# Graph attention stack on one core: layer 1's transposed input in another PSUM bank, and the context of layers 4 and 5 as three products of high and low halves

## What is computed

```
scores = where(adj == 0, -inf, q @ k.T * scale)
attn   = softmax(scores)
x      = layer_norm(x + (attn @ v) @ w + b) * gamma + beta
```

## Time and profile before

| | |
|---|---|
| median of 3 runs | 2370.72 us (2369.71 to 2372.63) |
| profiled execution, its own time | 2373.87 us |
| its span, first to last instruction | 2372.1 us |
| PE busy | 2259.9 us, 95% of the span |
| PE weight loads busy | 2136.2 us, 90% |
| DVE busy | 1783.3 us, 75% |
| POOL busy | 1794.9 us, 76% |
| ACT busy | 1620.0 us, 68% |
| mean granted TensorE clock | 0.990 of full speed |
| DMA | 68.78 MB, mean 29 GB/s |

### The profile page before, as it was taken

The page is one execution under the profiler, slowest core; times in us unless marked ns, Lnnn a source line. Parts: engine busy times, 40 slices in busy tenths (PEclk is TensorE's granted clock), DMA queues, the critical chain, the costliest instruction groups (busy, mean ns, idle before and its releaser), DMA issues.

```text
span 2372.1 us, 59576 instructions
## 1 busy us (share of the span) xinstructions
PE 2259.9 (95%) x20624; PEld 2136.2 (90%) x20624; DVE 1783.3 (75%) x7734; ACT 1620.0 (68%) x5515; POOL 1794.9 (76%) x2399
## 2 busy tenths in 40 slices
PE   6899999999999999999999999999999999999985
PEld 5799999999999999999999999999999999999974
DVE  4777777777877877877877877877777777777864
ACT  5667767767767767767767767766766766767742
POOL 3368878878878878878878878878878878878751
PEclk9999999999999999999999999999999999999998
DMA  4000000100110000010010000000010010000000
GB/s 154 20 23 24 30 28 24 30 28 25 29 28 25 29 28 26 28 28 26 28 28 27 27 28 28 26 28 28 26 28 28 26 28 28 26 29 17 15 10 14
DMA packets 38747, 68.78 MB, mean 29 GB/s; under 512 B 4400, under 2 KB 12848, under 8 KB 37936
## 3 DMA queue, kind: packets, MB, share of 16 engines
q1 hardware_dynamic: 38448, 64.97, 9.0%
HBM read 48.18 MB, written 16.78 MB: 27 GB/s over the span
## 4 chain that ended last, share of the span: by engine, by line
PE 80%; DVE 9%; ACT 7%; issue 2%; POOL 1%; DMA 0%; POOLq 0%; SPq 0%; DVEq 0%
PE value_bank L450 17%; PE qk_bank L442 16%; PE context_bank L595 9%; PE unit_bank L450 7%; PE unit_bank L442 7%; PE qk_bank L549 7%; PE score_bank L579 5%; ACT probs L676 5%; PE unit_bank L506 4%; PE unit_bank L518 3%; DVE scores L820 2%; PE score_bank L576 2%; PE score_bank L586 2%; DVE xT_lo L854 2%; DVE scores L860 1%
## 5 line engine op out<-in xcount | busy, mean ns | idle before, releaser
L1046 POOL TENSOR_TENSOR x<-y,rows 128x512 f32<-128x512 f32 x305 | 392.0, 1285 | 188.9 <-DVE y L913 188.9
L698 ACT CAST xT_hi<-qk_bank 128x512 fp32r<-128x512 f32 x320 | 187.7, 587 | 399.8 <-PE qk_bank L549 399.6
L676 ACT ACTIVATE probs<-scores,negmax 128x128 f32<-128x128 f32 x1024 | 399.1, 393 | 88.6 <-DVE negmax L820 88.6
L913 DVE TENSOR_SCALAR y<-y,mv,rstd 128x256 f32<-128x256 f32 x730 | 304.2, 459 | 191.6 <-POOL rstd L1030 191.3
L442 PE MATMUL qk_bank<-xT_hi,w_lo 128*128 128x256 f32 x1280 | 411.5, 321 | 21.6 <-DVE xT_lo L854 21.3
L1054 POOL TENSOR_TENSOR x<-x,rows 128x512 f32<-128x512 f32 x305 | 393.8, 1291 | 19.2
L450 PE MATMUL value_bank<-w_lo,xT_hi 128*128 128x256 f32 x1280 | 394.4, 308 | 0.0
L442 PE MATMUL qk_bank<-xT_lo,w_hi 128*128 128x256 f32 x1280 | 363.5, 284 | 0.0
L442 PE MATMUL qk_bank<-xT_hi,w_hi 128*128 128x256 f32 x1280 | 362.1, 283 | 0.0
L450 PE MATMUL value_bank<-w_hi,xT_lo 128*128 128x256 f32 x1280 | 361.8, 283 | 0.0
L450 PE MATMUL value_bank<-w_hi,xT_hi 128*128 128x256 f32 x1280 | 361.0, 282 | 0.0
(11 more groups left out here) (93 smaller groups left out, 6503.3 us busy)
## 6 DMA issues: line engine op xcount, KB each, us to landing
x0T<-xT_in SPq DMA_DIRECT2D x64, 256.0 KB, 3.0
x<-x_in SPq DMA_DIRECT2D x64, 256.0 KB, 3.0
out<-x_out SPq DMA_DIRECT2D x64, 256.0 KB, 2.3
adj<-adj_in SPq DMA_DIRECT2D x64, 128.0 KB, 2.2
late_weights<-w_in SPq DMA_DIRECT2D x2, 1024.0 KB, 7.1
rows<-rows_in SPq DMA_DIRECT2D x1, 1792.0 KB, 11.7
probs0T<-w_in SPq DMA_DIRECT2D x4, 256.0 KB, 4.2
x<-w_in SPq DMA_DIRECT2D x1, 1024.0 KB, 13.2
```

The lines of the kernel that those rows point to most:

```text
L676: e = act.activation(probs0[:, j, g, quad], scores0[:, j, g, quad], ACT.Exp, scale=-1.0, bias=negmax0[:, j, g, quad:quad + 1], accum_out=t ...
L913: m = dve.tensor_scalar(y[:, r, g], y[:, r, g], mv[:, r, g, 0:1], rstd[:, r, g:g + 1], ALU.subtract, ALU.mult)
L1046: pool.tensor_tensor(result(norm), y[:, NORM_AT[norm] % YS], row_of_each(f"gamma{layer}"), ALU.mult).then_inc(zg_ready, 1)
```

## The change

Two parts. First, layer 1's input is transposed into `unit_bank[0]` instead of `qk_bank`, so `transpose_x` for layer 1 no longer waits for `qk_ready`; it waits for DVE's first `row_max0` of the next group, which reads that bank. ACT's copy to `xT` becomes a step of its own, `move_xT`, behind `softmax`, and DVE's `split_lo` no longer waits for it. Second, the context of layers 4 and 5 is made of three fp32r products per graph. For this ACT's two copies, of v and of probsT, write the high halves, and DVE gets two new subtractions per item for the low halves: `split_v` (128x512) and `split_probsT` (128x256). PE's waits for v and probsT become waits for the low halves.

The core of the diff:

```diff
+def in_halves(i):
+    return item(i)[0] >= LAYERS - 2
...
+        def xT_bank(i):
+            return unit_bank[0] if item(i)[0] == 1 and NTH[i] > 0 else qk_bank
...
             def transpose_x(i):
                 layer, group = item(i)
                 wait_result(pe, source_of(i))
-                if NTH[i] > 0:
+                psum = xT_bank(i)
+                if psum is not qk_bank:
+                    pe.wait_ge(negmax0_ready, after_unit(min(group + 1, GROUPS - 1), 0))
+                elif NTH[i] > 0:
                     pe.wait_ge(qk_ready, NTH[i])
...
             def context(i):
-                pe.wait_ge(probsT_ready, after(i))
-                pe.wait_ge(v_ready, after(i))
+                wait_probsT_moved(i)
+                wait_values_moved(i)
...
+                    for left, right in ((probsT_hi, v_lo), (probsT_hi, v_hi), (probsT_lo, v_hi)):
+                        mm = pe.matmul(context_bank[:, g * D:(g + 1) * D], left[:, ring(i), g], right[:, ring(i), g],
+                                       start=right is v_lo, stop=left is probsT_lo)
...
-                act.copy(flat3(xT_hi[:, ring(i)]), qk_bank[:, :]).then_inc(xT_hi_ready, 1)
-                if layer == 1:
-                    act.copy(flat3(xT[:, :]), qk_bank[:, :]).then_inc(xT_ready, 1)
+                act.copy(flat3(xT_hi[:, ring(i)]), xT_bank(i)[:, :]).then_inc(xT_hi_ready, 1)
+
+            def move_xT(i):
+                act.wait_ge(xT_lo_ready, after(i))
+                act.copy(flat3(xT[:, :]), xT_bank(i)[:, :]).then_inc(xT_ready, 1)
...
-                if layer == 1:
-                    dve.wait_ge(xT_ready, group + 1)
-                else:
-                    dve.wait_ge(xT_hi_ready, after(i))
-                dve.tensor_tensor(flat3(xT_lo[:, ring(i)]), qk_bank[:, :], flat3(xT_hi[:, ring(i)]).bitcast(F32),
+                dve.wait_ge(xT_hi_ready, after(i))
+                dve.tensor_tensor(flat3(xT_lo[:, ring(i)]), xT_bank(i)[:, :], flat3(xT_hi[:, ring(i)]).bitcast(F32),
...
+            def split_v(i):
+                dve.wait_ge(v_hi_ready, IN_HALVES_AT[i] + 1)
+                dve.tensor_tensor(flat(v_lo[:, ring(i)]), value_bank[:, :], flat(v_hi[:, ring(i)]).bitcast(F32),
+                                  ALU.subtract).then_inc(v_lo_ready, 1)
+
+            def split_probsT(i):
+                dve.wait_ge(probsT_hi_ready, IN_HALVES_AT[i] + 1)
+                dve.tensor_tensor(flat(probsT_lo[:, ring(i)]), score_bank[:, 0:G * N],
+                                  flat(probsT_hi[:, ring(i)]).bitcast(F32), ALU.subtract).then_inc(probsT_lo_ready, 1)
...
                 if (group := due(i, 2)) is not None:
                     split_headsT(group)
+                if item(i - 1) and in_halves(i - 1):
+                    split_v(i - 1)
...
                 if item(i - 2):
                     finish_or_normalise(("item", i - 2))
+                if item(i - 1) and in_halves(i - 1):
+                    split_probsT(i - 1)
                 if (group := due(i, 2)) is not None:
```

More of the change, by code:

```diff
@@ L140 @@
 LATER_LEAD = 3
+def in_halves(i):
+    return item(i)[0] >= LAYERS - 2
+IN_HALVES_AT = {i: at for at, i in enumerate(i for i in ITEMS if in_halves(i))}
+IN_FULL_AT = {i: at for at, i in enumerate(i for i in ITEMS if not in_halves(i))}
 KEPT = [i for i in ITEMS if item(i)[0] > 1]
@@ L205, in gnn_stack @@
         v = sb("v", [RING, G, D])
+        v_hi = sb("v_hi", [RING, G, D], F32R)
+        v_lo = sb("v_lo", [RING, G, D], F32R)
+        probsT_hi = sb("probsT_hi", [RING, G, N], F32R)
+        probsT_lo = sb("probsT_lo", [RING, G, N], F32R)
         scores = sb("scores", [RING, G, N])
@@ L283, in gnn_stack @@
         v_ready = sem("v_ready")
+        v_hi_ready = sem("v_hi_ready")
+        v_lo_ready = sem("v_lo_ready")
         scores_in_psum = sem("scores_in_psum")
@@ L503, in transpose_probs0 @@
                 pe.wait_ge(probs0_ready, after_unit(group, j))
+                if j == 0 and group > 1:
+                    pe.wait_ge(xT_ready, group)
                 for g in range(G):
@@ L556, in project_qk, with wait_values_moved, wait_probsT_moved @@
                 pe.wait_ge(xT_lo_ready, after(i))
+                if xT_bank(i) is not qk_bank:
+                    pe.wait_ge(qk_ready, NTH[i])
+                elif layer == 1:
+                    pe.wait_ge(xT_ready, group + 1)
                 project(qk_bank, xT_hi[:, ring(i)], xT_lo[:, ring(i)], parts).then_inc(qk_in_psum, 1)
+            def wait_values_moved(i):
+                if in_halves(i):
+                    pe.wait_ge(v_lo_ready, IN_HALVES_AT[i] + 1)
+                else:
+                    pe.wait_ge(v_ready, IN_FULL_AT[i] + 1)
+            def wait_probsT_moved(i):
+                if in_halves(i):
+                    pe.wait_ge(probsT_lo_ready, IN_HALVES_AT[i] + 1)
+                else:
+                    pe.wait_ge(probsT_ready, IN_FULL_AT[i] + 1)
             def project_v(i, g):
@@ L594, in context @@
                 for g in range(G):
-                    mm = pe.matmul(context_bank[:, g * D:(g + 1) * D], probsT[:, ring(i), g], v[:, ring(i), g],
-                                   start=True, stop=True)
+                    if not in_halves(i):
+                        mm = pe.matmul(context_bank[:, g * D:(g + 1) * D], probsT[:, ring(i), g], v[:, ring(i), g],
+                                       start=True, stop=True)
+                        continue
+                    for left, right in ((probsT_hi, v_lo), (probsT_hi, v_hi), (probsT_lo, v_hi)):
+                        mm = pe.matmul(context_bank[:, g * D:(g + 1) * D], left[:, ring(i), g], right[:, ring(i), g],
+                                       start=right is v_lo, stop=left is probsT_lo)
                 mm.then_inc(context_in_psum, 1)
@@ L715, in move_v @@
                 act.wait_ge(v_in_psum, after(i))
-                act.copy(flat(v[:, ring(i)]), value_bank[:, :]).then_inc(v_ready, 1)
+                if NTH[i] >= RING:
+                    act.wait_ge(context_in_psum, after(i) - RING)
+                if in_halves(i):
+                    act.copy(flat(v_hi[:, ring(i)]), value_bank[:, :]).then_inc(v_hi_ready, 1)
+                else:
+                    act.copy(flat(v[:, ring(i)]), value_bank[:, :]).then_inc(v_ready, 1)
             def softmax(i):
@@ L726, in move_probsT @@
                 act.wait_ge(probsT_in_psum, after(i))
-                act.copy(flat(probsT[:, ring(i)]), score_bank[:, 0:G * N]).then_inc(probsT_ready, 1)
+                if in_halves(i):
+                    act.copy(flat(probsT_hi[:, ring(i)]), score_bank[:, 0:G * N]).then_inc(probsT_hi_ready, 1)
+                else:
+                    act.copy(flat(probsT[:, ring(i)]), score_bank[:, 0:G * N]).then_inc(probsT_ready, 1)
             def split_first(name):
@@ L758, in _ @@
                     softmax(i - 1)
+                if item(i) and item(i)[0] == 1:
+                    move_xT(i)
                 if item(i - 1) and late_values(i - 1):
```

9 lines of the change are left out of this document (5 added, 4 removed).

## The result

After the change the median is 2391.28 us (4 runs, 2390.9 to 2395.06) against 2371.68 (4 runs); the ratio of the means is 1.0087, 95% interval 1.0069 to 1.0104. The change costs 19.6 us; +15 was forecast (2386 from the median shown, range 2358 to 2400). The total is near. Two of its terms are not, as will be seen.

The account below looks back on a forecast made before the run. PE, 95% busy, was held once per period by a DVE, POOL and ACT chain to kT. +0.24 over about 60 periods (+14.4), start -0.4 and tail +1 gave +15: 2386 us (+0.6%), range 2358 to 2400.

Parts of the forecast that it names:

- The gate of kind 0's score: On PE, kind 0's score would wait for ACT's probsT copy instead of kT; the bank edit alone gains 0.12 or 0.07.
- the cold score: On PE, a score behind a wait takes 0.08 more until its results are there, besides 0.15 to start.
- The lateness in kind 3: On DVE, v_lo (0.09) and probsT_lo (0.35) make the group's residual 0.44 late, moving kind 0's score by +0.34 per period.
- PE's savings: Contexts in kinds 3 and 4 each 0.15 shorter, 0.30 per period, worth nothing because PE then waits longer.
- The sum per period: 0.34 lost less 0.10 gained, +0.24 per period over about 60 periods: +14.4 us.
- Kind 0 was to give 0.10: In kind 0, DVE's xT_lo no longer waits for the xT copy: 0.10 per period gained.
- The tail: Uncovered PE waits for probsT: the low half adds about 0.4 at three or four places, less shorter contexts: +1 us.
- The start: In the first two periods the transposes gain without the new DVE work: -0.4 us.
- the first (cover for the new subtractions): Both new DVE subtractions hide in waits, lateness 0, 0.20 gained in each of 60 periods: about 2359 us; chance 0.14.
- the second: One DVE subtraction hides or is half as long: lateness 0.2 to 0.3, 2371 to 2378 us; chance 0.17.
- the third: Transposes' 0.47 and contexts' 0.30 leave PE's path, 0.77 per period, 46 us in all: 2325 us; chance 0.05.
- the fourth: DVE instructions don't overlap, each costs its full length: lateness 0.67, 0.23 more per period, 2400 us; chance 0.04.

Follow-up runs that it names:

- the doubled subtraction: The whole change, with layer 4's DVE subtraction probsT_lo made twice, the first into a tile that nothing reads: 2411.51 us, ratio 1.0179 to the kernel before.
- the third kernel: Kernel before plus layer 1's input in its new bank and three-product contexts for layer 5 only: 2351.23 us, ratio 0.9919.
- the first: Kernel before with only layer 1's input in another bank and its later xT copy, every context one fp32 product: 2356.32 us, ratio 0.994.
- the halves alone: Kernel before with only the contexts of layers 4 and 5 as three products, layer 1's input in its old bank: 2404.84 us, ratio 1.0144.
- Reordered: The whole change, with DVE's probsT_lo ahead of the item's normalise from slot 316 on: 2384.79 us, ratio 1.0063 to the kernel before.

## Why the prediction was right, and where it was not

**The gate of kind 0's score.** Right: kT no longer holds the transposes, the score waits for probsT, and starts 0.14 after its copy (0.15 taken from the tail). The 0.08 for a score behind a wait is there too: from the score to the context behind it PE takes 1.24 now and 1.16 before.

**The lateness in kind 3.** Right almost to the digit. v_lo costs 0.60 and leaves add_residual 0.07 late (0.09 forecast). probsT_lo costs 0.33, the low end of 0.33 to 0.40 (0.35 taken). The group's residual comes 6.86 after the score (6.90 forecast), 0.40 later than in the long periods before (0.44 forecast) and 0.45 later than in the short ones. That nothing behind it has slack is shown by the doubled subtraction.

**PE's savings.** Right for the whole change: the sum of kinds 3 and 4 is the same with either form of layer 5's context. Not a law: with DVE's two steps away from kind 3, 0.16 of it counts in full, and that is the difference between the third kernel and the first.

**The sum per period was too large**, +0.24 against +0.13 and +0.16 measured (35.553 to 35.681, 35.493 to 35.657). Three terms, against which kind 1 took back 0.03 in the first pair and 0.01 in the second:

- The chain of kind 3 to kind 0 was made 0.05 too long. "In the other half the chain is now the same length" is right: after the change the stretch is 14.13 in every period. By the prediction's terms it is 14.18 (2059.32 + 0.15 - 2045.29). The surplus is in its prices: 0.61 where 0.60 was measured for each of the two 128x512 subtractions (headsT_lo and v_lo), 0.35 for probsT_lo where it was 0.33, and 0.15 for the score's start where it was 0.14.
- Kind 2 takes 7.84 in the long periods and 7.75 in the short ones. After, it takes 7.76 in all but one, so the long ones are gone with the change, worth 0.05 in the first pair and 0.02 in the second.
- Kind 0 was to give 0.10 against the 0.08 of the cold score, and gave 0.13 (context to second product 0.98, from 1.11): 6.04 instead of 6.10.

**The tail was the larger error**, +1 against +7.8 and +8.3. The failed step is "there the low half adds a subtraction and a semaphore". That is the price where DVE is idle, and it fits the waits of 0.82 and 0.81 (0.36 for the copy alone). It left out what stands ahead of the subtraction in DVE's list: a norm that waits for POOL's rstd. In the steady periods the same order is harmless to PE, since the score that needs probsT_lo comes after it; in the tail, without layer 0's work between, PE is there first. Reordered, 5 of the tail's 8 us came back (1.5 of them perhaps by the clock), and with no halves there all of it. The prediction had the rule in its hands, since it counted the same queue in kind 3, and did not apply it here.

**The start**, -0.4. The two pairs give +2.3 and +0.8, and over all twelve profiles the score of slot 22 lies between 194.39 and 201.36. Most of that scatter has arisen by the score of slot 10, before any context in halves is made, and it goes with the clock that TensorE was granted. In the first profile of the kernel before the clock first falls to half (1.2 of 2.4 GHz) at 35.9 us; PE had been busy 22.3 of the first 35 us.

| us at half clock ahead of the score of slot 10 | that score's start in the profiles with it |
|---|---|
| 17.1 | 107.71, 108.87, 108.88, 108.89 |
| 20.5 | 109.52, 111.00, 111.70 |
| 23.9 | 110.71, 110.73, 111.02 |
| 27.3 | 113.24 |
| 30.7 | 113.35 |

Which of the two causes the other is not shown. From slot 10 to slot 22 all twelve profiles have the same 3.4 us at half clock, and there the kernels do differ: 87.27 and 87.32 before, 88.06 and 88.09 after, 86.70 with the bank alone, 88.73 with the halves alone. So in this stretch the change costs 0.8 in both pairs; whether it gained 0.4 ahead of it can't be told.

So a steady term that was 5 to 7 us too large and a tail that was 7 too small nearly cancelled: that the total came so near is luck. Between the two profiled spans the change is 17.6 us, between the second ones 18.6, between the medians 19.6; what the forecast of 15 lacks beyond those two terms lies in the start and in the scatter of the runs. Of the rivals, the first (cover for the new subtractions) holds for layer 5's and not for layer 4's; the second is refuted by the lateness of 0.40, the third is refuted by the bank alone, the fourth by the doubled subtraction.

## What to carry to other kernels

An edit that shortens the bound engine's work is worth what the next gate behind it allows; find that gate, and the chain that feeds it, and price new work by whether it lies in that chain. The same edit can gain in one layer and lose in another: here, each with the bank, the halves of layer 5 alone gain 5 us and those of layer 4 alone lose 30, because of the slot in which another engine has to make them. Price a step at every place where it runs with what stands ahead of it in its engine's list, in the tail separately.

## What was not expected of the hardware

In the kernel before, slots of the same kind come in two lengths within one execution: kind 2 takes 7.75 or 7.84, kind 3 7.58 or 7.64. In its first profile 36 of 57 are long in either kind, in the second 12 and 18, and there kind 1 has two lengths as well, 7.67 and 7.72 to 7.74. In the long ones, runs of identical instructions take a few hundredths more. After the change the long kind 2 has all but vanished (one of 57, then none). What sets it was not found; it is not the granted clock, which is full from slot 22 to slot 307 in all twelve profiles.

The start differs by up to 7 us between profiles, and 5.6 of it is there by the score of slot 10, ahead of any half context. It goes with the time that TensorE spent at half clock, so a difference of a few us in the start of two single profiles should not be put down to an edit before the clock of both has been compared.
